# A transformer block on one core: the batch loop unrolled, the next batch's first tile multiplied in the last stage, and products of ones put into attention

## What is computed

```python
x = x + layernorm(attention(layernorm(x), Wq, Wk, Wv, Wo))      # 32 heads of 16, 8 key/value heads, rotary, causal
x = x + layernorm(moe(layernorm(x)))                            # 64 experts, 6 for each token, 128 rows each at most
# moe: scores = softmax(xf @ gate_w.T); topk_w, topk_idx = top_k(scores, 6)
#      each expert e: silu(x_e @ Wg_e) * (x_e @ Wu_e) @ Wd_e, times the score, added to its tokens' rows
#      plus a shared expert of width 384 for all tokens
```

## Time and profile before

| | us |
|---|---|
| median of the runs | 2201.94 |
| the profiled execution | 2224.34 |
| its span, to which all rows belong | 2222.6 |

### The profile page before, as it was taken

The page is one execution under the profiler, slowest core; times in us unless marked ns, Lnnn a source line. Parts: engine busy times, 40 slices in busy tenths (PEclk is TensorE's granted clock), DMA queues, the critical chain, the costliest instruction groups (busy, mean ns, idle before and its releaser), DMA issues.

```text
span 2222.6 us, 42066 instructions
## 1 busy us (share of the span) xinstructions
PE 1948.9 (88%) x12963; PEld 986.7 (44%) x12963; DVE 1315.7 (59%) x2863; ACT 1088.9 (49%) x1664; POOL 698.8 (31%) x985
## 2 busy tenths in 40 slices
PE   5999999979999999799999997989999969999930
PEld 3534435545344355453443554433435545555520
DVE  4679846636788466357984654579846512222248
ACT  2557773335577733355777333557763322222236
POOL 2212224632122246321222462212224622332245
PEclk9879999988799999887999998889999989999975
DMA  2122233310000022100000111000002359999978
GB/s 74 69 96 97 97 115 117 138 64 5 12 12 12 30 88 84 47 1 12 12 12 30 64 58 44 1 12 12 12 21 67 142 180 363 361 362 362 362 237 306
DMA packets 101223, 232.87 MB, mean 105 GB/s; under 512 B 23655, under 2 KB 23655, under 8 KB 92816
## 3 DMA queue, kind: packets, MB, share of 16 engines
q1 hardware_dynamic: 74160, 191.07, 23.2%
q0 software_dynamic: 24576, 35.07, 6.6%
q10 hardware_dynamic: 2272, 4.06, 0.5%
HBM read 141.59 MB, written 126.48 MB: 121 GB/s over the span
## 4 chain that ended last, share of the span: by engine, by line
PE 61%; DVE 11%; DMA 10%; issue 7%; ACT 3%; DVEq 2%; POOL 2%; another core or an unknown queue 2%; SPq 1%; POOLq 1%; ACTq 0%
PE ps L794 11%; DVE rmax L1309 8%; PE ps L733 8%; DMA ew_sb<-w_ew_dram 7%; PE ps L688 6%; PE ps L970 4%; PE ps L814 4%; PE ps L915 3%; PE ps L943 3%; PE ps L956 3%; PE ps L689 3%; PE ps L708 2%; PE ps L944 2%; PE ps L740 2%
## 5 line engine op out<-in xcount | busy, mean ns | idle before, releaser
L1309 DVE TENSOR_REDUCE rmax<-ps 128x1 f32<-128x512 f32 (+3 forms) x1280 | 732.4, 632 | 192.1 <-PE ps L743 115.0
L1121 ACT ACTIVATE pr<-ps 128x1024 f32<-128x1024 f32 (+3 forms) x768 | 587.0, 813 | 247.7 <-PE ps L814 240.6
L733 PE MATMUL ps<-kT,qT 48*128 48x512 f16 (+3 forms) x1536 | 399.2, 351 | 34.1 <-DVE rmax L1309 24.2
L794 PE MATMUL ps<-pr,v_ones 128*32 128x512 f32 (+3 forms) x3072 | 350.1, 531 | 3.1 <-ACT raw L1112 1.6
L1584 POOL TENSOR_SCALAR_AFFINE_SELECT pr<-pr 128x512 f32<-128x512 f32 x256 | 161.6, 636 | 512.3 <-ACT pr L1121 511.3
L814 PE MATMUL ps<-qT,kT 50*128 50x512 f16 (+3 forms) x1536 | 305.8, 348 | 12.4 <-DMA qT<-mT 7.3
L733 PEld LDWEIGHTS ps<-kT,qT 48*128 48x128 f16 x1536 | 123.0, 95 | 348.0 <-DVE rmax L1309 285.8
L1629 POOL DMA_INDIRECT dispatch_scratch<-x,slot_i x192 | 190.3, 991 | 72.4 <-issue 57.1
L970 PE MATMUL ps<-ew_sb,gxT 128*128 128x384 f32 x512 | 190.9, 496 | 8.2 <-DMA ew_sb<-w_ew_dram 8.2
L740 PE MATMUL ps<-above,sel 64*128 64x128 bf16 x1024 | 189.8, 226 | 0.0
L1648 POOL DMA_INDIRECT acc_scratch<-eo,etok x64 | 98.6, 1540 | 246.3 <-DVE eo L1451 219.7
(11 more groups left out here) (158 smaller groups left out, 2652.4 us busy)
## 6 DMA issues: line engine op xcount, KB each, us to landing
ew_sb<-w_ew_dram SPq DMA_DIRECT2D x64, 1152.0 KB, 10.2
dispatch_scratch<-blank SPq DMA_DIRECT2D x8, 2308.0 KB, 8.6
gx<-dispatch_scratch SPq DMA_DIRECT2D x64, 288.5 KB, 10.2
xin<-x_dram SPq DMA_DIRECT2D x32, 256.0 KB
acc_scratch<-blank SPq DMA_DIRECT2D x32, 256.0 KB, 2.1
xres<-x_dram SPq DMA_DIRECT2D x32, 256.0 KB
x_scratch<-x SPq DMA_DIRECT2D x32, 256.0 KB, 2.0
acc_scratch<-ysh SPq DMA_DIRECT2D x32, 256.0 KB
```

Source lines behind the costliest of these rows:

```text
L733: last = pe.matmul(o, qT[r:r + SROWS, half, 2 * g + h // 2, q % QPH * P:(q % QPH + 1) * P], kT[r:r + SROWS, g, kh * HALF:kh * HALF + w], s ...
L794: last = pe.matmul(ps[32 * h:32 * h + 32, 6, c0:HALF], v_ones[g % 2][:, kt, :], pr[i % SLOTS][:, h, 0:HALF - c0], start=kt == 0, stop=kt = ...
L1121: act.activation(pr[i % SLOTS][:, 2 * pair:2 * pair + 2, 0:HALF - c0], ps[:, 2 + 2 * pair:4 + 2 * pair, 0:HALF - c0], ACT.Exp, scale=facto ...
L1309: dve.tensor_reduce(dst[:, heads[0] % 2, heads[0] // 2:heads[0] // 2 + n, q % QPH], ps[:, BANK_OF[item], 0:n * w].rearrange("p (h k) -> p ...
```

## The change

All five loops over batches become Python loops, so `b` is a constant, the conditions on it go, and the lists are written out four times. The barrier `end_phase` at the end of each batch goes; the waits that it covered are named where they are needed (PE's transpose of tile 1 waits for `slot_ready`, its products for `ysh_ready`, POOL waits for its sent rows in step 1 of the next batch). In PE's step TT + 1 of the last stage stand the next batch's `x_transpose` of tile 0 and, behind x2's transpose, its `qkv_chunk` products. DVE's statistics of the next two tiles move to step TT - 2 and their normalising to TT - 1. `xT` and its neighbours move up in SBUF. In attention the rows go in two transfers of two rows; `ROWS` is 3.6; the planner counts its recent array work and orders `keep_warm` products, 128 rows by 512 columns of bfloat16 ones, ahead of "st" and "one" steps, into the bank that the step itself will overwrite, and behind the step's waits.

```diff
-    LAT, DRAIN, ROWS = 0.06, 0.17, 2.1
+    LAT, DRAIN, ROWS = 0.06, 0.17, 3.6
+    SPAN, ENOUGH, FILL, MOST = 3.42, 0.43, 0.214, 4
...
-        follow.insert(min(4, len(follow)) if g else 0, ("t1", g))
+        follow.insert(min(4 if g else 2, len(follow)), ("t1", g))
...
+    def fillers(at):
+        lo = at - SPAN
+        done = sum(part * max(0.0, min(end, at) - max(start, lo)) for start, end, part in runs[-40:])
+        return min(MOST, max(0, math.ceil((ENOUGH * SPAN - done) / FILL)))
...
+            n = fillers(at)
+            runs.append((at, at + n * FILL, 1.0))
+            at += n * FILL
             now["pe"] = at + (HALF - PUNITS[key[1]][2]) / 2400 + 0.006
             st[key] = now["pe"] + DRAIN
+            runs.append((at, now["pe"], 0.78))        # pv 1.0, one unit 0.37, stack 0.7
...
+                def keep_warm(bank, n):
+                    for _ in range(n):
+                        pe.matmul(ps[:, bank, :], ones_b[:], ones_b[:].unsqueeze(1).broadcast_to((P, HALF // P, P)),
+                                  start=True, stop=True)
...
-                    for part in range(2):
-                        for parity in range(2):
-                            row = ROWT * parity + SROWS + part
-                            sp.dma_start(qT[row:row + 1, half, bass.ds(2 * g, 2), :],
-                                         mT[half][16 * part + 8 * parity:16 * part + 8 * parity + 8, :]).then_inc(max_rows[half], 16)
+                    for parity in range(2):
+                        row = ROWT * parity + SROWS
+                        sp.dma_start(qT[row:row + 2, half, bass.ds(2 * g, 2), :],
+                                     mT[half][16 * parity:16 * parity + 16, :]).then_inc(max_rows[half], 16)
...
-            with pe.Fori(0, NB) as b:
+            for b in range(NB):
...
                     if t >= 1:
                         pe.wait_ge(xt_copied, n)
+                    if t == 1 and b >= 1:
+                        pe.wait_ge(slot_ready, TT * b)
+                    bank = XTB if t else 0
...
+                        if t == 1 and b >= 1:
+                            pe.wait_ge(ysh_ready, TT * b)
...
+                    if s == TT + 1 and b < NB - 1:
+                        x_transpose(b + 1, 0)
                     if 1 <= s - 2 < TT:
                         x2_transpose(s - 2)
+                    if s == TT + 1 and b < NB - 1:
+                        for c in range(DC):
+                            qkv_chunk(b + 1, 0, c)
...
-                end_phase(pe, b)
...
-                    if 1 <= s and s + 1 < TT:
+                    if 2 <= s and s + 1 < TT:
                         normalise(b, s + 1)
                     if 1 <= s <= TT:
                         rotate(s - 1)
+                    if s == 1:
+                        normalise(b, 2)
...
-                    if s == TT + 1:
-                        with dve.If(b < NB - 1):
-                            for t in range(2):
-                                stats(b + 1, t)
-                                normalise(b + 1, t)
-                end_phase(dve, b)
+                    if s == TT - 2 and b < NB - 1:
+                        for t in range(2):
+                            stats(b + 1, t)
+                    if s == TT - 1 and b < NB - 1:
+                        for t in range(2):
+                            normalise(b + 1, t)
```

More of the change, by code:

```diff
@@ L1 @@
+import math
 import numpy as np
@@ L139, in plan_attention @@
     stacked = {}
+    runs = []
     held = {bank: None for bank in BANKS}
@@ L284, in plan_attention @@
             now["pe"] = at + 0.61
+            runs.append((at, now["pe"], 0.7))
             turned[j] = now["pe"] + DRAIN
@@ L300, in plan_attention @@
             pv[key] = now["pe"] + DRAIN
+            runs.append((at + 0.18, now["pe"], 1.0))
             pe.append(("pv",) + key)
         else:
-            items = tuple(ring.pop(0) for _ in range(1))
+            items = (ring.pop(0),)
+            n = fillers(at) if what == "one" else 0
+            runs.append((at, at + n * FILL, 1.0))
+            at += n * FILL
             if what == "max":
@@ L668, in bank2, with x_transpose @@
                 return ps[:, 2 * k:2 * k + 2, :].rearrange("p a n -> p (a n)")
-            with pe.Fori(0, NB) as b:
-                def x_transpose(t):
+            for b in range(NB):
+                def x_transpose(b, t):
                     n = TT * b + t
@@ L811, in scores_transposed @@
                         pe.wait_ge(stack_copied, 3 * TT * (b + 1) - 3)
+                    keep_warm(2 + 2 * pair, fill)
                     for h in range(2):
@@ L870, in _ @@
                     else:
-                        ring(what[1])
+                        ring(*what[1:])
                 pe.wait_ge(pv_copied, 2 * KVH * (b + 1) + 1)
@@ L1040, in _, with copy_xT @@
             act.reg_load(factor, unscale[0:1, 0:1].bitcast(i32))
-            with act.Fori(0, NB) as b:
-                def copy_xT(t):
+            for b in range(NB):
+                def copy_xT(b, t):
                     act.wait_ge(xt_done, TT * b + t + 1)
-                    act.activation(xT[t % 2][:].rearrange("p c j -> p (c j)"), ps[:, 6, :], ACT.Copy).then_inc(xt_copied, 1)
+                    act.activation(xT[t % 2][:].rearrange("p c j -> p (c j)"), ps[:, 6 if t else 0, :],
+                                   ACT.Copy).then_inc(xt_copied, 1)
                 def copy_stack(t, j):
@@ L1141, in _ @@
                         copy_anT(s - 1, 2)
+                    if s == TT + 1 and b < NB - 1:
+                        copy_xT(b + 1, 0)
                     t = s - 2
@@ L1275, in _ @@
             dve.drain().then_inc(scale_ready, 1)
-            with dve.Fori(0, NB) as b:
+            for b in range(NB):
                 def rotate(t):
@@ L1537, in power, with all_sent @@
                 pool.tensor_tensor(rstd[:, k:k + 1], vr[:, k:k + 1], minus_half[:, 0:1], ALU.pow).then_inc(rstd_ready, 1)
+            def all_sent(b):
+                for k in range(4):
+                    wait_apart(pool, sent[k], 16 * TOPK * (TT // 4) * (b + 1))
+                pool.sem_inc(rows_sent, 1)
             power(0, 0)
             power(0, 1)
-            with pool.Fori(0, NB) as b:
+            for b in range(NB):
                 def lows(t):
@@ L1574, in _ @@
                         power(b, s + 2)
+                    if s == 1 and b:
+                        all_sent(b - 1)
                 def copy_v(g):
@@ L1632, in _ @@
                                 oob_is_err=False).then_inc(sent[t % 4], 16)
-                    if s == TT + 1:
-                        with pool.If(b < NB - 1):
-                            power(b + 1, 0)
-                            power(b + 1, 1)
-                for k in range(4):
-                    wait_apart(pool, sent[k], 16 * TOPK * (TT // 4) * (b + 1))
-                pool.sem_inc(rows_sent, 1)
-                wait_apart(pool, phase_end, (b + 1) * ENGINES)
+                    if s == TT - 2 and b < NB - 1:
+                        power(b + 1, 0)
+                        power(b + 1, 1)
+                if b == NB - 1:
+                    all_sent(b)
             end_late_phase(pool, 0)
```

67 lines of the change are left out of this document (31 added, 36 removed).

## The result

| | median, us (runs) | profiled execution, us | its span | mean granted clock |
|---|---|---|---|---|
| before | 2206.24 (20) | 2224.34 | 2222.6 | 0.926 |
| changed | 2187.38 (20) | 2186.59 | 2184.9 | 0.953 |

The ratio of changed to before is 0.9917, with a 95% interval of 0.9899 to 0.9936: 19 us faster. 2133 was predicted, and 2187 lies outside the range. The two profiled executions differ by 37.7 us, twice what the medians do.

What follows compares the result with a forecast made beforehand. PE was taken to set the pace nearly everywhere, losing time idle or at half clock at seams and attention's start. Seams 36 + exit 4 + `sgm` 3 + clock 42 - products 16 = 69 us; 2202 - 69 = 2133, range 2097 to 2180.

Steps and rivals of the forecast that it cites:

- The seams: Between batches: tile 0's work in the last stage fills PE's idle time; 12 us at each of three, 36 us.
- Behind the last batch: At the loop's exit, 4.00 us on POOL's queue go with the loop (4 us); half the late `sgm` adds 3.
- `sgm`'s wait: On ACT behind the last batch, `sgm` starts 5.6 us late; half taken as gained, 3 us, between 0 and 5.6.
- Attention's clock: Start and end of attention: added products keep PE's clock up, 42 us gained, less 16 us for the products.
- The ceiling: Most that attention's clock could return: 46 us in start stretches at DVE's undisturbed 0.889 share, 10 at the ends; 56.
- The price: Added products in attention at 0.214 us each, 37 a batch, 32 us if all on the path; half taken, 16.
- A: Rival on attention: the clock still falls, added products cost 16 us and give nothing back; 2175 us, chance 0.17.
- B: Rival on the seams and tail: the late `sgm` stays, seams give 8 instead of 12; 2148 us, chance 0.17.
- C: Rival: the new order and products slow attention's undisturbed heads, 68 us on the path; 2227 us, chance 0.06.
- D: Rival: all is won, seams 41, tail 10, attention 56 less 8, 99 us; 2103 us, chance 0.13.
- E: Rival: waits the barrier had hidden use up the seam's gain, attention neutral; about 2198 us, chance 0.06.
- The offset: Whole kernel: runs are 1% shorter than the profiled execution, and the same was taken off the forecast, 2155 to 2133.

Runs made afterwards that it cites:

- e6: Kernel before with only its batch loop written out on every engine, barriers and all else kept: 2188.91 us, ratio 0.9923.
- e10: Changed kernel without the added products and with tile 0's work back at the start of the next batch: 2183.34 us, ratio 0.9895.
- e1: Changed kernel without the 120 added products, all else kept: 2175.23 us, ratio 0.984.
- e13: Kernel before, unchanged, run again for a second profile: 2214.63 us, ratio 1.0002.
- e14: Changed kernel, unchanged, run again for a second profile: 2192.6 us, ratio 0.9899.
- e5: Changed kernel with tile 0's transposes, products and copy back at the head of the next batch: 2188.45 us, ratio 0.9924.
- e12: Changed kernel without added products, with an early one-column Exp and the next batch's tile 2 brought into the last stage: 2163.41 us, ratio 0.9807.
- e11: Changed kernel with an early one-column Exp and every added product doubled, 60 a batch: 2193.28 us, ratio 0.9947.
- e4: Kernel before with all of the change in attention (order, added products, two-row transfers), loops and barriers kept: 2198.07 us, ratio 0.9948.
- e15: Changed kernel with an early one-column Exp and its added products of 64 columns instead of 512: 2175.34 us, ratio 0.9827.
- e9: Changed kernel with the planner's products out, an early one-column Exp, and 18 products a batch ahead of step TT's items: 2184.04 us, ratio 0.99.
- e3: Changed kernel with a one-column Exp in QKV step 3 of batches 1 to 3, bringing the table load early: 2182.5 us, ratio 0.9871.
- e7: Changed kernel without the added products and with the early one-column Exp: 2172.96 us, ratio 0.9845.

## Why the prediction was wrong, step by step

The ratios build the change up from parts: written out 0.9923 (e6), with the barriers gone and attention's order, rows and layout 0.9895 (e10), with tile 0 in the last step 0.984 (e1), with the products 0.9917. In microseconds of 2206: -17, -6, -12 and +17. The 6 is within the intervals of the two runs that it is the difference of.

**The seams: size right, causes mixed up.** 36 us were forecast and 37.3 measured (31.8 between the second profiles, e13 and e14). Of the 37.3, e6 alone gives 23 (18 against e13's seams), where I had 10.4 for the jumps; the barriers give 4 (e6 less e10), tile 0's place gives 13.7 (e10 less e1), and the products take 3.5 back (e1 against the changed kernel). The good sum is luck in part, for its shares were wrong: had only one of the changes been made, my number for it would have been off.

**A cost left out: 4.9 us on the way to attention.** Tile 2 comes 9 us behind tile 1 instead of 6.6, and in the same batches POOL has a stall of 4.1 us ahead of its first `mb`, as it had before. The way to attention is 1.6 us longer there; in e5, e10 and e12, where tile 2 is not late, it is 57.3 us as before. That the late tile brings the stall into the open is argued, not shown: with tile 2 just as late, batch 3 of e1 and batches 1 and 2 of e11 lose nothing (57.3).

**Behind the last batch: wrong, small.** The 4.00 us of the earlier trace rows did not go with the loop; they are 3.99 us at the last barrier, written out (L534). The whole tail, from tile 5's output on, is 2.2 us shorter (0.3 between the second profiles), not 7. `sgm`'s wait ahead of it, of which I had taken half, stays too: 6.56 us.

**Attention's clock, the term that failed: 42 us less 16 were forecast, and 2.9 came in the first pair of profiles, -8 in the second.** Three things in it:

1. The ceiling. I scaled DVE's time to its share in undisturbed heads, and so took all of the difference for low clock. At a clock of 0.96 (e4) the start stretch still takes 87.3 us, with DVE at 0.83. Against 88.3 to 92.2 in both profiles of before that is 1 to 5 us a batch. On the stretch of the earlier trace rows e4 saves 22 us in all against the first profile and 17 against the second, with the products' price and the two transfers in it, where I had put a ceiling of 46 and taken three quarters. e4's whole attention is 23.5 us below the first profile of before and 17 below the second, and that in the fastest of its runs.
2. The price. A product takes 0.49 us in the mean and not 0.21 to 0.29: 0.38 even at full clock, and about 0.6 where it runs at 1.2 GHz, behind the fall at 98 us first of all. All of them are 53 us, of which I took half of 32. e15 shows that the products' length is the price and e11 that it grows with their number. e9 shows that an earlier place makes it worse.
3. The table load, which writing out moved. With the products it costs 5 us (e3); without them nothing (e7).

**The rivals.** A (products cost, nothing comes back, 2175) named the right mechanism for the time, though not for the clock, which rises by 0.016; its number is 12 us below the measured one. B was half right: `sgm`'s wait is still there when the kernel is only written out (8.25 us in e6), so the loop is not its cause. The Trainium skill (Runtime: NRT & Kernel Launch, Instruction fetch mechanics) says that fetches in straight-line code are mostly hidden; the trace agrees in so far as no instruction transfer runs during this wait in any of the four batches of the kernel before. Where the wait comes from stays open. In the changed kernel it stands once (6.6 us, last batch) instead of four times; with tile 0 back at its old place (e10) it stands four times again, 7.9 to 8.5 us, so tile 0's work in the last step is what removes it.

The Trainium skill (TensorE: Matmul & The Clock Gate, What's actually happening) ties the lower clock to an idle engine. e9 does not speak against that, and the prediction misread how its own products act: it said that products behind waits close no gap, but PE, busy 3.48 of 5 us from 93 to 98 us in e7, is busy for all 5.00 in e9, and there the clock is still at 0.94 from 98 to 106 us.

C is refuted: the undisturbed heads take 25.8 us as before. D is refuted by attention. E (2198) was right that attention is neutral, but the seams' gain was not used up.

**The offset** between profile and median was taken over as 1%, and did not hold: before it is 2224 against 2206, changed it is nothing (2187 against 2187), and in the second profile of before it is nothing either (2213 against 2215). The first profile of before is an outlier of its kernel, which is why the profiles differ by 37.7 us and the medians by 19.

## What to carry to other kernels

Price a clock gain by a stretch of the same kernel at the high clock, not by another stretch's share of busy time, and set against it every product that buys it, at the lower clock's duration if the clock is down where it stands, and ask which engine sets the pace there (in e9 it was DVE). When a loop is written out, look at what stood at its head (a table load, first instructions) and where it lands. If a calculated seam names its next late part (here tile 2), mend that part too: it brought 8 to 10 us here (e12).

## What was not expected of the hardware

Between kernels the mean granted clock says nothing of the time: 0.938 at 2173 us (e7), 0.963 at 2193 (e11). Within one kernel the two go together: e4's runs go from 2184 us at 0.959 to 2207 at 0.950. 0.009 of the clock means that 0.018 of the span, 39 us, is at half rate instead of full, which loses 20 us of work; 23 were measured.

Writing a loop out removes more than its jump: 6 to 8 us at each of three seams, where the chain showed 3.47. In the first seam the trace splits the gain: 4.3 us are PE's idle time while instruction transfers run, and 2.9 us are the same products at a higher clock behind the shorter pause (e6).
